# Pair comparison as eight tensor-scalar operations on VectorE, and the node features loaded through ScalarE's queue

## The reference, cut to what matters

```
# layer 0, per edge e
a   = tanh(relu(sum((x[src] @ A1.T + b1) * (x[dst] @ A2.T + b2 + rel_emb[etype])) / sqrt(32)))
msg = sum_b w_comp[etype, b] * (x[src] @ weight[b])           # 16 bases
nei = segment_sum(a * msg, dst)
out = relu(where(in_degree > 0, nei + x[src[last edge of dst]] @ self_loop, 0))
# layer 1: segment_sum(x[src], dst)
# layer 2: attention softmax over the edges of each dst, then a weighted sum of x[src]
# layer 3: ten steps f = 0.9 * D_dst A D_src f + 0.1 * f0, with A the count of edges per (dst, src)
```

## Time and profile before

| | us |
|---|---|
| median of three runs | 1178.94 |
| lowest and highest run | 1175.4, 1184.0 |
| the profiled execution | 1179.21 |
| its span, first to last instruction | 1177.4 |

### The profile page before, as it was taken

One profiled execution on the slowest core, in us unless ns is written; L12 is line 12 of the kernel. 1 busy time (PEld: TensorE's weight loads), 2 busy tenths in 40 slices (PEclk: granted clock), 3 DMA queues, 4 the chain that ended last, 5 costly groups with the idle time before them and its releaser, 6 DMA issues.

```text
span 1177.4 us, 55398 instructions
## 1 busy us (share of the span) xinstructions
PE 896.5 (76%) x23682; PEld 846.3 (72%) x23682; DVE 929.4 (79%) x1684; ACT 507.7 (43%) x1244; POOL 640.4 (54%) x580
## 2 busy tenths in 40 slices
PE   3358887868688768776787777767376968999996
PEld 2357877767587667776776677766376968999996
DVE  8869999978798879887888787887647996555556
ACT  0235655444554447664756566656458410000000
POOL 5777777777777777777777787877000000000000
PEclk9568999987798889888878888889587989999998
DMA  4432322322233223222322223231000000000001
GB/s 114 60 72 55 63 59 54 64 55 45 51 56 55 53 45 60 49 53 50 60 47 54 49 55 62 44 55 29 4 3 2 4 3 4 4 5 4 4 5 18
DMA packets 54911, 47.93 MB, mean 41 GB/s; under 512 B 35966, under 2 KB 45182, under 8 KB 54662
## 3 DMA queue, kind: packets, MB, share of 16 engines
q0 software_dynamic: 18176, 9.34, 9.7%
q1 hardware_dynamic: 30822, 14.16, 5.8%
q10 hardware_dynamic: 5664, 20.84, 4.8%
HBM read 41.98 MB, written 2.31 MB: 38 GB/s over the span
## 4 chain that ended last, share of the span: by engine, by line
POOL 42%; PE 23%; DVE 16%; issue 15%; DMA 2%; ACT 2%; DVEq 0%; ACTq 0%; SPq 0%
POOL arena L633 42%; PE ps L885 13%; PE ps L932 3%; DVE arena L1373 2%; PE ps L916 2%; PE ps L856 2%; PE ps L895 2%; DVE aggT L1417 1%; DMA arena<-line_table 1%; ACT arena L1122 1%; DVE arena L1368 1%; DVE arena L1404 1%; DMA arena<-rel_rows_in 1%; DVE arena L1388 1%; PE ps L818 0%
## 5 line engine op out<-in xcount | busy, mean ns | idle before, releaser
L633 POOL DMA_INDIRECT arena<-x_pad,arena x568 | 638.5, 1124 | 173.4 <-issue 173.1
L818 PE MATMUL ps<-aggT 128*128 128x128 f16 x3024 | 230.1, 247 | 44.3 <-DVE aggT L1417 44.3
L818 PEld LDWEIGHTS ps<-aggT 128*128 128x128 f16 x3024 | 216.5, 114 | 49.0 <-DVE aggT L1417 49.0
L1404 DVE TENSOR_TENSOR arena<-ps,arena 128x1536 f32<-128x1536 f32 x98 | 172.4, 1759 | 3.4
L885 PE MATMUL ps<-arena,adj_words 128*128 128x64 f16 x5625 | 171.9, 192 | 3.3 <-DVEq L1666 3.2
L885 PEld LDWEIGHTS ps<-arena,adj_words 128*128 128x128 fp8e4 x5625 | 170.5, 97 | 4.6 <-DVEq L1666 3.5
L1075 ACT ACTIVATE adj_words<-arena 128x500 uint8 x196 | 126.5, 645 | 56.6 <-ACT arena L1050 54.9
L780 PE MATMUL ps<-arena 128*32 128x44 f32 (+4 forms) x7048 | 134.5, 215 | 20.2 <-DVE arena L1404 20.0
L1045 ACT ACTIVATE arena<-ps 128x500 fp8e4<-128x500 f32 x196 | 113.0, 577 | 79.0 <-PE ps L767 79.0
L780 PEld LDWEIGHTS ps<-arena 128*32 128x32 f32 x7048 | 110.5, 115 | 43.8 <-DVE arena L1404 26.7
L1373 DVE TENSOR_TENSOR arena<-pair_no,arena 128x2400 bf16<-128x2400 f16 x98 | 137.3, 1401 | 0.0
(11 more groups left out here) (222 smaller groups left out, 1153.2 us busy)
## 6 DMA issues: line engine op xcount, KB each, us to landing
arena<-line_table ACTq DMA_DIRECT2D x48, 344.0 KB
arena<-x_pad,arena POOLq DMA_INDIRECT x568
arena<-pick_table SPq DMA_DIRECT2D x27, 256.0 KB
arena<-line_table ACTq DMA_DIRECT2D x48, 80.0 KB
arena<-dst_parts SPq DMA_DIRECT2D x196, 5.7 KB
agg_table<-arena SPq DMA_DIRECT2D x196, 2.5 KB
dst_parts<-aggT SPq DMA_DIRECT2D x1, 735.0 KB
x<-x_pad SPq DMA_DIRECT2D x1, 400.0 KB
```

What stands on the lines that cost most here:

```text
L633: pool.indirect_dma_start(to, None, table, bass.IndirectOffsetOnAxis(ap=index, axis=0)).then_inc(done, 16)
L818: mm = nc.tensor.matmul(ps[:, at:at + PICK_WIDE * FEAT], pick_hot[:, u % PICK_RING, k * P:(k + 1) * P], x_parts[:, t, j * PICK_WIDE:(j + 1 ...
L1404: v.tensor_tensor(mixed[:, d % 2, :, :, 0:BASES], fetched_of(d)[:, :, SCORED:REL_COLS].unsqueeze(2).to_broadcast(n), weighted.unsqueeze(3) ...
```

## The change

The pair comparison of a duo, one tensor-tensor of 2400 elements on each partition, becomes eight tensor-scalar operations, one for each slot, with the edge's pair number as a per-partition scalar in f32. Each writes only the columns that `count` reads: 200, 275, 275 and 300 elements, twice. `pair_twice` and its copy are dropped; `pair_of` (f32, as large) takes its place. The eight operations are spread: three between the product and the sum of the scores, three behind the sum, two behind the row comparison. The steps that were linked in the sweep (product and sum, the three steps of the picked rows, weighting and mixing) have other operations between them now. `make_lines` moves behind `make_mixed`, and `make_dst_hot` and the first `make_pick_hot` stand ahead of the small comparison, the other pick units behind the weighting.

In the prelude `x` is loaded through ScalarE's DMA queue with a semaphore of its own, `x_loaded`; TensorE's transposes and VectorE's uses of `x` wait for it alone. The large part of the target table is stored through ScalarE's queue, behind its copies, instead of SyncE's.

```
-        pair_twice = stay.cut(2 * GROUPS * SLOTS, F16)...
+        pair_of, dst_off, last_off_1 = [stay.cut(GROUPS * SLOTS)... for _ in range(3)]
...
-            loads = [(x[:], x_pad.rearrange("(b p) f -> p b f", p=P)), (a12[:, 0:FEAT], a1_t), ...
+            loads = [(a12[:, 0:FEAT], a1_t), ...
...
-            sp.dma_start(by_block[:, FIRST_STORED:BLOCKS], q_parts[:, FIRST_STORED:BLOCKS]).then_inc(parts_stored, 16)
...
         def _(pe):
-            pe.wait_ge(inputs_loaded, 16 * LOADS)
+            pe.wait_ge(x_loaded, 16)
             pe.wait_ge(constants_made, CONSTANTS)
             (transposes of x)
+            pe.wait_ge(inputs_loaded, 16 * LOADS)
...
         def _(act):
+            act.dma_start(x[:], x_pad.rearrange("(b p) f -> p b f", p=P)).then_inc(x_loaded, 16)
             act.wait_ge(inputs_loaded, 16 * LOADS)
+            act.wait_ge(x_loaded, 16)
...
             last.then_inc(rows_made, 1)
+            act.wait_ge(parts_split, 1)
+            act.dma_start(dst_parts...[:, FIRST_STORED:BLOCKS], q_parts[:, FIRST_STORED:BLOCKS]).then_inc(parts_stored, 16)
...
-            link(v.tensor_copy(pair_twice, pair_whole.unsqueeze(3).to_broadcast([P, GROUPS, SLOTS, 2])))
...
-                    n = [P, WIDE, HOTS * BLOCKS // 2, 2]
-                    v.tensor_tensor(pair_hot[:, h]..., pair_no[:]..., slots_of(pair_twice, d)...,
-                                    ALU.is_equal).then_inc(pairs_ready, 1)
+                def make_pairs(d, k0, k1):
+                    if k0 == 0 and d >= 2:
+                        dve.wait_ge(pairs_used, (d - 1) * DUO)
+                    for k in range(k0, k1):
+                        n = PAIR_DSTS[k % SLOTS] * BLOCKS
+                        last = v.tensor_scalar(pair_hot[:, d % 2, k, 0:n], pair_no[:, 0:n],
+                                               pair_of[:, d * DUO + k // SLOTS, k % SLOTS:k % SLOTS + 1], None, ALU.is_equal)
+                    if k1 == WIDE:
+                        last.then_inc(pairs_ready, 1)
...
                 for d in range(DUOS):
-                    score_edges(d)
-                    if d + 1 < DUOS:
-                        make_pairs(d + 1)
-                    (lines, dst_hot, read_picked, pick_hots, make_mixed)
+                    c, own = d // LINE_DUOS, UNITS_AT.get(d, [])
+                    picked_now, more = PICK_READ_AT.get(d), d + 1 < DUOS
+                    products_of(d)
+                    if more:
+                        make_pairs(d + 1, 0, 3)
+                    scores_of(d)
+                    if more:
+                        make_pairs(d + 1, 3, 6)
+                    if picked_now is not None:
+                        mask_picked(picked_now)
+                    if more:
+                        make_rows(d + 1)
+                    if picked_now is not None:
+                        add_halves()
+                    if more:
+                        make_pairs(d + 1, 6, WIDE)
+                    if picked_now is not None:
+                        add_pairs(picked_now)
+                    if d % LINE_DUOS == 1 and c + 1 < LINES:
+                        make_dst_hot(c + 1)
+                    for n in own[0:1]:
+                        make_pick_hot(*n)
+                    make_last(d)
+                    weigh(d)
+                    for n in own[1:]:
+                        make_pick_hot(*n)
+                    make_mixed(d)
+                    if d % LINE_DUOS == 0 and c >= 1 and c + 1 < LINES:
+                        make_lines(c + 1)
```

More of the change, by code:

```diff
@@ L472, in gnn @@
         result_ready, stored = sem("result_ready"), sem("stored")
-        LOADS = 14
+        LOADS = 13
         EDGE_LOADS = 5
@@ L1361, in slots_of, with make_rows @@
                     return per_slot[:, d * DUO:(d + 1) * DUO]
[L1363 to L1366, removed]
+                def make_rows(d):
                     n = [P, WIDE, P // 2, 2]
-                    v.tensor_tensor(row_hot[:, h].rearrange("p k (v i) -> p k v i", i=2),
+                    v.tensor_tensor(row_hot[:, d % 2].rearrange("p k (v i) -> p k v i", i=2),
                                     row_no[:].rearrange("p (v i) -> p v i", i=2).unsqueeze(1).to_broadcast(n),
@@ L1387, in score_edges, with scores_of, make_last @@
                         dve.wait_ge(gathered[d % AHEAD], 16 * tiles)
-                    link(v.tensor_tensor(product, fetched_of(d)[:, :, 0:SCORED], xp[:, d % AHEAD], ALU.mult))
+                    step(v.tensor_tensor(product, fetched_of(d)[:, :, 0:SCORED], xp[:, d % AHEAD], ALU.mult))
+                def scores_of(d):
+                    chain.wait()
                     v.tensor_reduce(score[:, d % 2, :], product, AX.X, ALU.add).then_inc(score_ready, 1)
-                def make_mixed(d):
-                    at = d % LINE_DUOS * WIDE
-                    own_hot = dst_hot[:, d // LINE_DUOS % 2, at:at + WIDE, :]
+                def make_last(d):
                     if d >= 2:
@@ L1399, in make_mixed, with weigh @@
                                     ALU.is_equal)
+                def weigh(d):
+                    at = d % LINE_DUOS * WIDE
                     dve.wait_ge(weight_ready, d + 1)
-                    link(v.scalar_tensor_tensor(out=weighted, in0=weight_e[:, d % 2, :].unsqueeze(2).to_broadcast(n),
-                                                scalar=0.0, in1=own_hot, op0=ALU.max, op1=ALU.mult))
+                    step(v.scalar_tensor_tensor(out=weighted,
+                                                in0=weight_e[:, d % 2, :].unsqueeze(2).to_broadcast([P, WIDE, HOTS]), scalar=0.0,
+                                                in1=dst_hot[:, d // LINE_DUOS % 2, at:at + WIDE, :], op0=ALU.max, op1=ALU.mult))
+                def make_mixed(d):
+                    chain.wait()
                     n = [P, WIDE, HOTS, BASES]
@@ L1426, in read_picked, with add_halves @@
                                          pick_mask[:, c].rearrange("p k w -> p (k w)").unsqueeze(2).to_broadcast(n), ALU.mult))
+                def add_halves():
+                    half = PICK_WIDE // 2
+                    chain.wait()
                     dve.sem_inc(pick_read, 1)
-                    of = picked.rearrange("p (k w f) -> p k w f", k=WIDE, w=PICK_WIDE)
-                    half = PICK_WIDE // 2
-                    link(v.tensor_tensor(of[:, :, 0:half], of[:, :, 0:half], of[:, :, half:PICK_WIDE], ALU.add))
@@ L1431, in read_picked, with add_pairs @@
-                    link(v.tensor_tensor(xp[:, PICKED[c] % AHEAD, :, 0:FEAT], of[:, :, 0, :], of[:, :, 1, :], ALU.add))
+                    step(v.tensor_tensor(picked_of[:, :, 0:half], picked_of[:, :, 0:half], picked_of[:, :, half:PICK_WIDE], ALU.add))
+                def add_pairs(c):
+                    chain.wait()
+                    step(v.tensor_tensor(xp[:, PICKED[c] % AHEAD, :, 0:FEAT], picked_of[:, :, 0, :], picked_of[:, :, 1, :], ALU.add))
                 make_lines(0)
                 make_dst_hot(0)
-                make_pairs(0)
+                make_rows(0)
```

35 lines of the change are left out of this document (13 added, 22 removed).

## The result

The changed kernel takes 1150.62 us (median of four runs, 1147.62 to 1152.06), the kernel before 1180.76 beside it; the ratio is 0.9743, with a 95% interval of 0.9711 to 0.9775. Faster by 2.6%: 30 us, where 42 were forecast. The profiled execution has a span of 1147.6 us (before 1177.4).

A forecast was written before the change was run, and what follows sets the result against it. GpSimd's gathers were taken to bound the sweep after VectorE's first sixth, 101 us of it being stretch. From 1179.2 us, 44 less for gathers and 2 more at the sweep's end gave 1137 us, range 1112 to 1166.

The forecast's parts named there:

- GpSimd's gathers bound the sweep, and their stretch is what can be won: Sweep: 568 gathers on GpSimd decide its end; 101 us of it are gathers stretched beyond 0.945 us.
- The pair comparison on VectorE, 0.25 us a duo more: Pair comparison on VectorE: eight short operations take 1.57 us a duo in place of 1.32, hidden by the gathers.
- The lower bound: Pair comparison on VectorE: with only 0.067 us fixed per operation, 1.08 us a duo, 0.24 less than before.
- The spreading, 0.3 us a duo: VectorE's sweep: operations put between linked steps remove waiting bubbles, saving 0.3 us a duo.
- the three bubbles: VectorE's linked pairs: 0.11 us at the scores, 0.09 at the weighting, 0.09 in the picked duos' steps.
- What GpSimd takes from VectorE, 0.2 us a duo: Pair operations on VectorE: 115 new operations lose 0.15 us each to GpSimd's hold, 0.2 us a duo.
- The gathers, 44 us: GpSimd's gathers in the sweep: stretch falls from 101 to 57 us, the last gather issued 44 us earlier.
- The end of the sweep, 2 us: Behind the last gathered row: duo 97's pairs come about 1.8 us later, then counts, copies and tanh; 2 us added.
- The prelude, nothing: Ahead of the sweep: earlier `x`, transposes and moved store price at 0, lying under GpSimd's gathers from 11.0 us.
- VectorE as the bound: Rival, VectorE in the sweep: at 7.6 us a duo it becomes the bound, 1158 us; chance 0.13.
- Dear operations: Rival, `make_pairs`: 784 short operations cost about 0.3 us or more each, sweep slower, 1226 us at 0.35; chance 0.08.
- Strings that block as a whole: Rival, gathers: strings of short operations block like one long one, 115 gathers by 0.6 us, 1179 us; chance 0.09.

The follow-up runs named there:

- Without gathers: Changed kernel, kernel before, and eight operations in the old place, each without gathering source rows of duos 11 to 97: 1093.57, 1087.07 and 1108.02 us.
- 18 or 34 gathers fewer: Changed kernel with 29 or 31 picked duos in place of 27: 1131.58 us (ratio 0.9582) and 1120.37 us (ratio 0.9497).
- the eight in the old place: Kernel before with only the pair comparison made eight tensor-scalar operations, in one string where it stood: 1147.13 us, ratio 0.9728; also run without most gathers, 1108.02 us.
- 31 picks: 31 picked duos in place of 27: on the changed kernel 1120.37 us, on the eight operations in the old place and order 1136.66 us.
- The last experiment: Changed kernel with its eight pair operations in one string behind sum and masking, row comparison between product and sum: 1129.87 us, ratio 0.9554.

## Why the prediction was right, and by how much it was off

The forecast was 1137 in a range of 1112 to 1166, faster; measured were 1150.6. Step by step:

- **GpSimd's gathers bound the sweep, and their stretch is what can be won.** Right. Without gathers the same work ends 55 us earlier; 18 or 34 gathers fewer give 19 or 30 us; and the whole gain stands in the last gather's start, 791.3 against 821.4.
- **The pair comparison on VectorE, 0.25 us a duo more.** Right: 0.23 by the kernels without gathers. The eight take 0.20 us each, 1.6 together; the 1.8 us worked out beside it from the fixed term of the page "VectorE: DVE Perf Modes" of the Trainium skill was not seen. (The lower bound had a fixed part of 0.067 us; 1.32 less 2400 times 0.52 ns is 0.07. Nothing hangs on it.)
- **The spreading, 0.3 us a duo.** Half: 0.16. In the new order VectorE waits longer for ScalarE's tanh: without gathers 18.9 us in all, where it is 1.8 with the eight in the old place, 0.17 us a duo. With that added back the spreading is at 0.33, about what I gave the three bubbles. I had priced the tanh at 0 to 0.1 us a duo and left it out of the 0.3. It cost nothing, being hidden under the gathers; with 31 picks it isn't.
- **What GpSimd takes from VectorE, 0.2 us a duo.** Far too much: the pair operations keep VectorE busy 3.3 us longer with the gathers than without, 0.03 us a duo. It was hidden too.
- **The gathers, 44 us.** This is the term that was mis-sized: 31 us (101 to 70), and the 13 us between are what the forecast missed the time by. Gathers that began inside pair operations lost 21 us (17 forecast). A pair operation by itself costs less than I took: 35 gathers ended 0.82 us behind the end of one, and they lost 0.08 us each (0.15 forecast). But 24 began so close ahead of the row comparison that this held them as well, 15.6 us; I had not thought of what stands next to the short operations. Gathers that began inside the lines comparison lost 4 us (8 forecast), inside the row comparison 13 (18 before). What I left out altogether are gathers caught in mid-flight, 12 us, by the lines comparison in its new place. I had read from the trace that a pick comparison beginning 0.5 us after a gather doesn't stretch it, and took the start of a gather as its only open moment. The row that said otherwise was in my hands: the gather of 403.76 ended with a string of one-input operations.
- **The end of the sweep, 2 us.** 0.5 us: 12.3 us from the landing to the last mixing product, 11.8 before. ScalarE's tanh came later by less than the pairs did.
- **The prelude, nothing.** Right. The reason for it was partly off: `x` landed only at 13.54 us, 12.8 us after its issue, while six other loads of up to 392 KB were issued beside it, so the transposes began 5.1 us earlier and not 8; VectorE's first edge input came 1.3 us later (13.33 against 12.03).
- **The rivals.** VectorE as the bound: no, without gathers it is done 55 us earlier. Dear operations: no, 0.20 us each. Strings that block as a whole: refuted for the pair operations, since the eight in one string in the old place gave the full gain; but where lines and pick comparisons stand together they blocked as one each of the gathers that they caught under way with the lines moved back.

The kernels sort as follows. The form of the comparison gives the 30 us. In the new order the move of the lines gives 10 us (1160.9 to 1150.6) where the rest of the new order, with the lines behind the pairs, is 14 us worse than the old order with the same eight operations (1160.9 against 1147.1). That fits the pair operations standing on both sides of the row comparison: with them taken away from it, 1129.9, and the 15.6 us of gathers that it caught behind a pair operation are gone. The last experiment moved three things at once (one string, the rows ahead of it, the masking ahead of it), so how much of its time each gives stays open.

## What to carry to other kernels

When an engine that never waits still takes longer for the same instruction from time to time, lay its timeline beside those of the other engines and sort the long ones by what ran when they began, and also by what ran when they ended. Here the costly thing was not how long VectorE's operations were in sum but which of them stood next to each other: eight short operations cost VectorE more and the kernel less, and their order alone was then worth 21 us more. Before a string of operations is blamed as a whole, count behind which of them the long ones come out. And what a change is worth depends on which engine is the bound: the new order was worth nothing at 27 picks and 16 us at 31, so shift the work between the engines before judging such a change.

## What the runs showed of the hardware

- A gather on GpSimd's queue, 0.945 us undisturbed, has at least two moments at which VectorE can hold it. At its start it is held by a comparison that runs then, with two inputs in SBUF or with one, and ends 0.82 us behind the end of that comparison: in the kernel before the 55 that began in a row comparison and the 26 that began in a pick comparison. Later it was held by lines and pick comparisons, and came out 0.12 us behind the end: 427.43 behind 427.31, and 431.53 behind 431.41. Two-input comparisons were not seen to hold it there: the 55 of the row comparison ended 0.82 us behind it although the two-input pair comparison followed at once.
- The later moment lies 0.47 to 0.49 us behind the start: in the changed kernel the lines comparisons that began 0.27 to 0.47 us behind a gather's start held it, all 37, while the 12 gathers of the kernel before that had been under way for 0.49 us when a pick comparison began were not stretched.
- Of one-input operations in a string the short ones hardly count: in the changed kernel none of the 46 gathers that met a pair operation at 0.48 us was stretched, with the eight in one string away from the row comparison 4 of 24 were, by up to 0.21 us. And a string isn't always one block: in the kernel before 28 of 69 gathers held under way came out 0.12 us behind the first of two pick comparisons, the other 41 behind the last operation of the string. What tells the two apart stays open.
- The Trainium skill's page "SBUF — State Buffer", in the section on which engine shares ports with which, has two inputs keeping GpSimd from reads and the two-port modes keeping it from both until they end. The first agrees with the row comparison; of the second the lines and pick comparisons show it, with 0.12 us behind the end, and the pair operations, if they run in such a mode, do not show it under way.
- Short one-input operations on 200 to 300 elements of 16 bits follow one another in 0.20 us, with 200 or 275 elements as with 300.
- A load of 400 KB issued at 0.74 us on ScalarE's queue landed 12.8 us later, while SyncE issued six others from 0.74 us on, five of them of 392 KB.
